# Keys of two heads side by side: the 64-row products behind a decoder block's cross-attention scores

## What is computed

```python
x = x + attn(layernorm(x))       # distance attention over the first axis (4 long), 16 heads of 16
q = (layernorm(x) @ Wq + bq)     # per head h: 512 x 64
k = (ctx @ Wk + bk)              # per head h: 64 keys x 64
v = (ctx @ Wv + bv)
x = x + softmax(q @ k.T / 8) @ v @ Wo + bo
x = x + moe(layernorm(x))        # 8 experts, each takes its 256 best rows; gelu(xin @ W1 + b1) @ W2 + b2
```

## Time and profile before

| | |
|---|---|
| median of 3 runs | 424.45 us (422.96 to 425.5) |
| the profiled execution's own time | 424.85 us |
| its span in the trace | 423.1 us |
| mean granted TensorE clock | 0.904 of full |
| PE, PEld, DVE, ACT, POOL busy | 327.0, 290.5, 310.0, 189.3, 204.2 us |

### The profile page before, as it was taken

One profiled execution on the slowest core, in us unless ns is written; L12 is line 12 of the kernel. 1 busy time (PEld: TensorE's weight loads), 2 busy tenths in 40 slices (PEclk: granted clock), 3 DMA queues, 4 the chain that ended last, 5 costly groups with the idle time before them and its releaser, 6 DMA issues.

```text
span 423.1 us, 6126 instructions
## 1 busy us (share of the span) xinstructions
PE 327.0 (77%) x2169; PEld 290.5 (69%) x2169; DVE 310.0 (73%) x699; ACT 189.3 (45%) x340; POOL 204.2 (48%) x239
## 2 busy tenths in 40 slices
PE   0786968487988899999999973111399999999991
PEld 0674756374666799999999972000299989999991
DVE  3069899996557889888888854887447787789950
ACT  3346465245554464756666454100032565452330
POOL 3706875951111336588887878200214235524622
PEclk9969799979999999999999996555579999999997
DMA  8920000000000003412531535200026577612322
GB/s 261 381 82 2 2 0 2 0 0 0 0 2 0 2 12 126 135 56 110 161 102 38 174 121 181 85 1 0 25 57 200 144 224 208 177 20 45 51 26 25
DMA packets 24046, 34.26 MB, mean 81 GB/s; under 512 B 1785, under 2 KB 20561, under 8 KB 23889
## 3 DMA queue, kind: packets, MB, share of 16 engines
q1 hardware_dynamic: 20112, 29.36, 21.2%
q0 software_dynamic: 3072, 4.20, 5.5%
q10 hardware_dynamic: 832, 0.32, 0.4%
HBM read 27.58 MB, written 6.29 MB: 80 GB/s over the span
## 4 chain that ended last, share of the span: by engine, by line
PE 53%; DVE 25%; DMA 7%; POOL 5%; issue 5%; ACT 4%; POOLq 0%; DVEq 0%; ACTq 0%
PE bank L838 13%; PE bank L839 12%; PE bank L840 12%; DMA xg<-xn_rows,idx 6%; DVE flags_all L1171 3%; PE bank L859 3%; PE bank L805 2%; DVE stats L525 2%; PE bank L1289 2%; DVE dist L608 2%; DVE G_lo L537 1%; PE bank L901 1%; PE bank L1319 1%; DVE H_lo L824 1%; DVE acc L567 1%
## 5 line engine op out<-in xcount | busy, mean ns | idle before, releaser
L1379 POOL DMA_INDIRECT xg<-xn_rows,idx x16 | 20.1, 1259 | 85.6 <-DVE idx L1453 83.2
L1349 ACT ACTIVATE hbuf<-bank,b_cols 128x256 f32<-128x256 f32 x64 | 26.9, 472 | 55.5 <-PE bank L840 51.9
L961 POOL TENSOR_TENSOR prob<-prob,rsum 128x1024 f32<-128x1024 f32 x16 | 30.5, 1906 | 21.3 <-DVE rsum L1055 19.8
L838 PE MATMUL bank<-xgT_hi,W_hi 128*128 128x256 f32 x128 | 37.3, 291 | 1.4 <-DVE xgT_lo L1443 1.4
L838 PE MATMUL bank<-H_hi,PT_hi 128*128 128x256 f32 x128 | 36.3, 284 | 1.7 <-DVE PT_lo L1032 1.7
L838 PE MATMUL bank<-W_hi,h_hi 128*128 128x256 f32 x128 | 37.3, 292 | 0.0
L839 PE MATMUL bank<-xgT_lo,W_hi 128*128 128x256 f32 x128 | 37.1, 290 | 0.0
L840 PE MATMUL bank<-xgT_hi,W_lo 128*128 128x256 f32 x128 | 37.0, 289 | 0.0
L840 PE MATMUL bank<-H_hi,PT_lo 128*128 128x256 f32 x128 | 36.2, 283 | 0.0
L839 PE MATMUL bank<-H_lo,PT_hi 128*128 128x256 f32 x128 | 36.2, 283 | 0.0
L840 PE MATMUL bank<-W_hi,h_lo 128*128 128x256 f32 x128 | 36.2, 282 | 0.0
(11 more groups left out here) (230 smaller groups left out, 1028.4 us busy)
## 6 DMA issues: line engine op xcount, KB each, us to landing
W_raw<-in_L_ffn_W SPq DMA_DIRECT2D x16, 1024.0 KB, 5.2
X<-in_x SPq DMA_DIRECT2D x4, 512.0 KB, 9.1
xn_rows<-xn SPq DMA_DIRECT2D x16, 128.0 KB, 1.8
out_x<-X SPq DMA_DIRECT2D x4, 512.0 KB, 3.8
Wq<-in_L_xattn_Wq SPq DMA_DIRECT2D x1, 1024.0 KB, 9.2
Wk<-in_L_xattn_Wk SPq DMA_DIRECT2D x1, 1024.0 KB, 11.8
Wv<-in_L_xattn_Wv SPq DMA_DIRECT2D x1, 1024.0 KB, 15.2
Wo<-in_L_xattn_Wo SPq DMA_DIRECT2D x1, 1024.0 KB, 11.9
```

What stands on the lines that cost most here:

```text
L838: t.matmul(out_ps, hi, rhs_hi, start=first, stop=False)
L961: g.tensor_tensor(prob[:, s], prob[:, s], rsum[:, s].unsqueeze(2).to_broadcast([P, HX, CK]), ALU.mult).then_inc(prob_ready, 1)
L1349: ins = a.activation(hbuf[:, g % 2, f % 2], banks[g][:, (f % 2) * CAP:(f % 2 + 1) * CAP], ACT.Gelu_apprx_tanh, bias=b1_cols[:, e * FC + f: ...
L1379: g.indirect_dma_start(xg[:, s, h], None, xn3_dram, bass.IndirectOffsetOnAxis(ap=idx[:, e, h:h + 1], axis=0), bounds_check=ROWS - 1, oob_i ...
```

## The change

The keys no longer stand block-diagonally. `kT` holds them as they come out of the key product: 256 columns (4 batches x 64 keys), one head in rows 0 to 63 and the other in rows 64 to 127. A chunk's G is then four products of 64 rows by 256 columns instead of two of 128 rows by 512: for each half m of the features, one product in the upper half of the array's rows and one in the lower. Each head has a PSUM bank, and the two halves m lie side by side in it. The memset of `kv_bd` goes, and ACT copies a chunk's keys with one instruction instead of two. `G_hi` and `G_lo` are laid out with the feature half outside the batch, so that one evacuation takes a bank as 8 pieces of 64 columns; the first-layer weights that share this memory are laid out alike. Both banks are waited for before the chunk's first product.

```diff
-        kv_bd = region([("kv_bd", [P, 2, CB, 2, CK], F32)])
+        kT = region([("kT", [P, 2, CB * CK], F32)])
...
-            [("G_hi", [P, CB, MC, HK], F32R), ("G_lo", [P, CB, MC, HK], F32R)],
-            [("W1_hi", [P, 4, MC, F], F32R), ("W1_lo", [P, 4, MC, F], F32R)],
+            [("G_hi", [P, MC, CB, HK], F32R), ("G_lo", [P, MC, CB, HK], F32R)],
+            [("W1_hi", [P, MC, 4, F], F32R), ("W1_lo", [P, MC, 4, F], F32R)],
...
+        by_chunk = lambda bank: v3(bank[:], MC * CB)
+        def of_head(G, c, h):
+            return G[:].rearrange("p m b n -> p (m b) n")[:, :, c * P + h * DK:c * P + (h + 1) * DK]
...
-            g.tensor_scalar(trials_f[:, :, 3], trials_f[:, :, 1], 3.0, None, ALU.mult)
-            g.memset(kv_bd[:], 0.0).then_inc(consts_ready, 1)
+            g.tensor_scalar(trials_f[:, :, 3], trials_f[:, :, 1], 3.0, None, ALU.mult).then_inc(consts_ready, 1)
...
-                for h in range(2):
-                    s = slice(h * DK, (h + 1) * DK)
-                    a.activation(kv_bd[s, c % 2, :, h, :], v3(ps[s, 0:CB * CK], CB), ACT.Identity,
-                                 bias=bias_cols[s, NC + c:NC + c + 1]).then_inc(kv_ready, 1)
+                a.activation(kT[:, c % 2], ps[:, 0:CB * CK], ACT.Identity,
+                             bias=bias_cols[:, NC + c:NC + c + 1]).then_inc(kv_ready, 1)
...
-                for m in range(MC):
-                    ps = bank_full(act, f"G{c}{m}")
-                    a.activation(G_hi[:, :, m, c * P:(c + 1) * P], v3(ps[:], CB), ACT.Copy,
-                                 scale=DK ** -0.5).then_inc(G_hi_ready, 1)
+                for h in range(2):
+                    ps = bank_full(act, f"G{c}{h}")
+                    a.activation(of_head(G_hi, c, h), by_chunk(ps), ACT.Copy, scale=DK ** -0.5).then_inc(G_hi_ready, 1)
...
-                pe.wait_ge(kv_ready, 2 * (c + 1))
-                kT = kv_bd[:, c % 2].rearrange("p b h k -> p (b h k)")
+                pe.wait_ge(kv_ready, c + 1)
+                ps = [bank_free(f"G{c}{h}") for h in range(2)]
                 for m in range(MC):
-                    ps = bank_free(f"G{c}{m}")
-                    filled(t.matmul(ps[:], WqT[:, c, m * P:(m + 1) * P], kT, start=True, stop=True), f"G{c}{m}")
+                    for h in range(2):
+                        rows = slice(h * DK, (h + 1) * DK)
+                        mm = t.matmul(ps[h][:, m * CB * CK:(m + 1) * CB * CK], WqT[rows, c, m * P:(m + 1) * P],
+                                      kT[rows, c % 2], start=True, stop=True)
+                        if m == MC - 1:
+                            filled(mm, f"G{c}{h}")
...
-            sp.dma_start(W1_raw[:, e % PLACES],
+            sp.dma_start(W1_raw[:, :, e % PLACES],
```

More of the change, by code:

```diff
@@ L438, in K_evac @@
                 ps = bank_full(act, f"KT{c}")
[L439 to L440 removed]
                 if c >= 2:
[L442 removed]
+                    b, n, _ = where[f"G{c - 2}1"]
                     act.wait_ge(full[b], n + 1)
[L444 to L447 removed]
+                a.activation(kT[:, c % 2], ps[:, 0:CB * CK], ACT.Identity,
+                             bias=bias_cols[:, NC + c:NC + c + 1]).then_inc(kv_ready, 1)
             def K_ahead(c):
@@ L531, in low_parts @@
             def low_parts(c):
[L533 to L537, removed]
-                                           in1=raw(G_hi[:, :, m, s]), op0=ALU.mult, op1=ALU.subtract).then_inc(G_ready, 1)
+                for h in range(2):
+                    ps = bank_full(dve, f"G{c}{h}")
+                    dve.wait_ge(G_hi_ready, 2 * c + h + 1)
+                    v.scalar_tensor_tensor(out=of_head(G_lo, c, h), in0=by_chunk(ps), scalar=DK ** -0.5,
+                                           in1=raw(of_head(G_hi, c, h)), op0=ALU.mult,
+                                           op1=ALU.subtract).then_inc(G_ready, 1)
             def WqT_evac(k):
@@ L1002, in W_high @@
                 act.wait_ge(W1_loaded[p], 16)
-                nc.scalar.activation(W1_hi[:, p, part], W1_raw[:, p, part], ACT.Copy).then_inc(W1_hi_ready, 1)
+                nc.scalar.activation(W1_hi[:, part, p], W1_raw[:, part, p], ACT.Copy).then_inc(W1_hi_ready, 1)
             else:
@@ L1013, in W_low @@
                                           (W2_raw, W2_hi, W2_lo, W2_hi_ready, W2_ready))
+            at = (slice(None), part, p) if j < 2 else (slice(None), p, part)
             pool.wait_ge(hi_ready, 2 * e + j % 2 + 1)
-            nc.gpsimd.tensor_tensor(lo[:, p, part], W[:, p, part], raw(hi[:, p, part]),
-                                    ALU.subtract).then_inc(ready, 1)
+            nc.gpsimd.tensor_tensor(lo[at], W[at], raw(hi[at]), ALU.subtract).then_inc(ready, 1)
         def dve_step(dve, k, order):
@@ L1361, in act_part4 @@
                     for m in range(MC):
-                        a.activation(W1_hi[:, p, m], W1_raw[:, p, m], ACT.Copy).then_inc(W1_hi_ready, 1)
+                        a.activation(W1_hi[:, m, p], W1_raw[:, m, p], ACT.Copy).then_inc(W1_hi_ready, 1)
                     act.wait_ge(W2_loaded[p], 32)
@@ L1415, in W_low_late @@
                 dve.wait_ge(hi_ready, 2 * (e + 1))
-                v.tensor_tensor(lo[:, p], W[:, p], raw(hi[:, p]), ALU.subtract).then_inc(late, 1)
+                at = (slice(None), slice(None), p) if layer == 1 else (slice(None), p)
+                v.tensor_tensor(lo[at], W[at], raw(hi[at]), ALU.subtract).then_inc(late, 1)
             def onehot_of(x):
```

12 lines of the change are left out of this document (6 added, 6 removed).

## The result

| | before | after |
|---|---|---|
| median (lowest to highest, runs) | 424.84 us (422.77 to 425.73, 14) | 427.86 us (424.59 to 431.73, 14) |
| ratio of the medians, 95% interval | | 1.0072 (1.0047 to 1.0097) |
| the profiled execution's own time | 424.85 us | 428.27 us |
| its span | 423.1 us | 426.5 us |
| mean granted TensorE clock | 0.904 | 0.895 |

The change is slower by 0.7%. The slowest of its 14 executions, 431.73 us, stands apart from the rest and is left out of the ratio. The median is 4.2 us above the forecast and 1.7 above the upper end of the range.

The account below looks back on a forecast made before the run. Part 1's chain of waits was taken to bound the change: GpSimd and ACT first, DVE to 100 us, then PE and ACT. Terms -0.95, -1.5, +0.2, +1.4, -0.4 sum to -1.25; forecast 423.7 us, range 421.7 to 426.2.

Parts of the forecast that it names:

- Costed at nothing: List of effects priced at zero: high and low parts, scores, first-layer weight layout, and no instruction added in parts 2 to 4.
- Or if parts 2 to 4 change length: One of the signs, listed in advance, that would show the prediction wrong in the changed kernel's profile.
- The memset, -0.95: Start of part 1: without GpSimd's memset, block 1's scale and all behind it come 0.95 us sooner.
- The clock behind it, -1.5: 22 to 28 us: PE's shorter gap probably avoids the fall to half clock, saving 1.5 us (ends 0 and 1.7).
- rival 2: Part 1: the early clock fall comes all the same, and the one at 100 us too; 425.1 us, chance 0.13.
- The key copy and G: Each chunk: one key copy of 0.47 us, 0.48 less; G in five slots, 1.07 us instead of 1.72.
- Taken 0: Each chunk's two switches between 128-row and 64-row products: 0 to 0.33 us each at half clock, counted as nothing.
- Rival 3: Chunks 5 to 7: 64-row products don't overlap and each switch drains; 3.3 us dearer, 427.0 us, chance 0.11.
- DVE's chain covers chunks 0 to 4: Part 1, about 28 to 100 us: DVE's own work sets the time, so savings in these chunks count as nothing.
- Chunk 5's early wait, +0.2: Chunk 5: both G products now wait for the low part of G40, so `y_product` starts 0.2 us later.
- the fall behind it, +1.4: About 100 us: PE idles longer ahead of chunk 5's G, the clock falls, costing 1.4 us (ends 0 and 2.5).
- Chunks 6 and 7, -0.4: End of part 1: shorter G closes up ACT's copies, so the first H product starts 0.4 us sooner.

Follow-up runs that it names:

- e6: The changed kernel with 96 small unused matmuls (192 PE records) added in part 3, so part 4's instruction packets fall as before: 423.97 us.
- g4: The same kernel as e6, measured on another occasion: 424.05 us.
- e7: The kernel before with 32 small unused matmuls (64 PE records) in part 3 and nothing of the change: 429.35 us.
- e4: The changed kernel with five unused matmuls ahead of chunk 5's G products, where PE otherwise idles: 427.27 us.
- e1: The kernel before with only the memset of `kv_bd` moved behind block 1's scale and shift on GpSimd: 421.83 us.
- f1: e1 with block 3's transposes, mix copies and `y_product` moved ahead of chunk 5's G: 422.74 us.
- g1: e4 with 86 small unused matmuls in part 3, which put part 4's instruction packets back: 424.49 us.
- g3: e5 with e6's 96 small unused matmuls in part 3: 423.05 us.
- f3: The changed kernel with 96 small unused matmuls in part 3, and block 3's transposes and `y_product` ahead of chunk 5's G: 420.42 us.
- e5: The changed kernel with a chunk's G products ordered by head, each bank waited for just ahead of its own head's products: 426.00 us.
- e8: The changed kernel with 2 KB left free beside `kT`, so later buffers keep the addresses they had before: 426.22 us.

## Why the prediction was wrong

**The step that failed** is "In parts 2 to 4 no instruction is added", under *Costed at nothing*. It is true of those parts, and it was taken to mean that they cannot change. What the change adds is 64 records in part 1 of PE's stream, and they moved the instruction packets of part 4 into two gathers. In the profiled executions that is 1.8 us. In the medians it is more: 3.9 and 3.8 us between the change and e6, g4, and 4.8 between before and e7. A part of this surplus is falls of the clock behind a longer wait, as in e4 at 355 us and in e7 at 358 (the profiled execution of the change has none there); another part may be chance in part 1 of the executions, since the profiled one of the change has a fall at 61 us that e6 and g4 have not. How it divides is not settled. With the packets back in place the change measures 424.0 against 424.6, a difference of -0.6. The sum had -0.75 against the median. "Or if parts 2 to 4 change length" was one of the forecast's own signs of being wrong, and it is the one that came.

The other half of the profiled loss is in part 1: +1.73 us at the first H product, where the sum had -1.25. It is in the terms below, most of it falls of the clock; the profiles of e6 and g4, the same instructions in part 1, have -1.01 and -0.69 there.

Point by point:

- *The memset, -0.95*: right. ACT starts 0.97 us sooner.
- *The clock behind it, -1.5*: right where it stayed up (e1, e4, f1, g1, g3, g4, f3: copies at 25.2), missing in the change, e5, e6 and e8 (26.6 to 26.8). The forecast looked at the gap of 2.3 us that it closed, and not at the one of 1.24 that opened behind it, in which PE waits for two small ACT copies. But the gap alone does not decide: it is 1.23 to 1.25 us in all the profiles but that of before, and the clock stayed up behind it in seven. "PE's work ahead of that gap hangs on transfers and stays put" was wrong too, since its end lies anywhere from 18.8 to 20.5 us. The fall was rival 2's case, and so was the one at 99 us (425.1); it costs 1.4.
- *The key copy and G*: 0.47 and 1.07 us as taken. The 1.07 came out for the wrong reason. All four pairs overlap, in either program order where both banks are free, and each of two switches costs 0.2 us, half of it on the neighbouring product. "Taken 0" for a switch was wrong within its bounds of 0 to 0.33, and "the low end needs another order" was wrong.
- *Rival 3, no overlap and drains*: not what made it slower, since the pairs do overlap, though its switches are there at 0.2 instead of 0.33 us.
- *DVE's chain covers chunks 0 to 4*: right for DVE, whose waits from 30 to 100 us sum to 2.6 us in both kernels. Missed was GpSimd: its pair sums wait for PE's transposes of the mix, so the slow query product at 61.52 came out on the path, 0.8 us. e6 and g4 had the same gap ahead of that product (2.99 and 2.98 us) and no fall, so this term is not one of the change in every execution. In e4, e5, f1 and f3 a fall half as long there, 3.4 us, cost nothing at the low part of G40.
- *Chunk 5's early wait, +0.2, and the fall behind it, +1.4*: 0.3 and 1.9, right in kind. The fall came in two of the four profiles of the change with its own order of waits (the change and g4, not e6 and e8).
- *Chunks 6 and 7, -0.4*: didn't come, 10.49 against 10.45. G7's two products wait for the second bank, which DVE empties behind block 3's statistics. e5 and g3, which ask for one bank at a time, have the gain: 9.94 and 9.95.

In the chances, slower by over 0.5% had 0.11, all of it from rival 3; no rival was about a part that the change leaves alone.

## What to carry to other kernels

Adding or removing instructions early in PE's stream moved the packets in which all later ones are fetched; where the path goes through gathers that share the DMA engines, compare how long each gather takes to land and whether an instruction packet lies within it before a difference is put down to the change, and try a padded version. A change that makes PE faster under cover of another engine buys idle time, and every fall of part 1 in these profiles began in a stretch in which PE was idle or less than 2 us behind one: look at the gap that opens behind the one that closes. Wait for each bank just ahead of the product that fills it; two waits ahead of the first product cost the change 0.3 us at chunk 5, and 0.5 us in chunks 6 and 7, which was all that the shorter G had gained there.

## What was not expected of the hardware

- **Instruction packets and gathers.** A packet of 16 KB comes every 12 to 20 us of part 4, and an expert takes about 14, so it meets the same place for several experts in a row. Of the gathers that the chains show at 320 to 370 us, those without a packet inside landed in 5.0 to 6.0 us and those with one in 6.1 to 6.8. The packet itself is 1% of the engines' time, so it is not its share of the bandwidth. By what it holds the gather up wasn't tried.
- **The clock differs between executions of one kernel.** After much the same 2.97 and 2.99 us of gap it fell in one and not in the other, and a fall sets how long the next gap is. Without the slowest, the change's runs lie 5.7 us apart, those of before 3. The Trainium skill ("TensorE: Matmul & The Clock Gate", Part 1) says that the number of slow matmuls at a kernel's start varies from run to run; the traces agree, with 4.00 us for the first query product in one profile and 5.06 in another. They add that on a chain of dependent steps the falls that counted cost 0.8, 1.4 and 1.9 us. What decides an execution's falls stays open.
- **Row halves.** Two products of 64 rows in the two halves of the array start 6 to 14 ns apart (33 to 37 behind an idle stretch of PE) and run at the full pace of 0.216 us for a record of 256 columns, whichever comes first in the program (e5, chunk 5, shows one series starting between records of the other); going over to them and back costs 0.2 us each.
